# Paged attention in pairs of rounds instead of single rounds

## The chip, the core and the metric

The kernel runs on one core of a Trainium2 chip, in one launch. What is measured is the device time of that launch in microseconds; lower is better. TensorE (PE) multiplies matrices, VectorE (DVE) and ScalarE (ACT) do arithmetic on tiles, GpSimd (POOL) issues the gathers, and SyncE (SP) issues the other transfers.

## The reference, cut to what matters

The whole model is a state-space convolution, a causal attention, an attention over a paged cache, and a feed-forward layer with LoRA. The change touches only the paged attention:

```python
q, k, v = x @ Wq.T, x @ Wk.T, x @ Wv.T     # 32 entries of 32 tokens, 32 query heads, 8 key heads, D = 128
q, k = rope(rmsnorm(q)), rope(rmsnorm(k))
k_all = concat([k_cache[block_table], k])  # 16 pages of 32 keys, and 32 new keys: 544 keys
v_all = concat([v_cache[block_table], v])
scores = einsum(q, k_all) * SCALE          # four query heads to each key head
scores = where(valid, scores, -1e30)
o = softmax(scores) @ v_all
out = o @ Wo.T
```

Everything is float32.

## The kernel before, in words

`cached_attention` (lines 1232 to 1612) works on one batch entry and one key head at a time. That is a round: 128 query rows (4 heads of 32 tokens) against 544 keys. An entry has 8 rounds (k = 0 to 7), and a loop body has two entries, 16 rounds (i = 0 to 15); it is written out once for m = 0 and then looped 15 times. There are 256 rounds in all. Each engine has its own order of work, and semaphores join them.

A round passes through these steps:

- `split_hi` (ScalarE, L1401) copies the keys to a high part, and `split_lo` (VectorE, L1490) takes the rest as a low part. There are two buffers for each. At k = 1 and k = 4 the queries of the entry are split too (L1400 with 384 and 512 columns, L1487). Round k = 0 isn't split; it is multiplied in float32 (L1551).
- `scores` (TensorE, L450 to L452) has six matmuls: three products for each of two parts of the keys. The scores of even and odd rounds lie in one tile of three PSUM banks and share the middle bank. So each round computes its end part first, then waits until the mask of the round before is done, then computes its middle part.
- `mask_scores` (VectorE, L1501) adds the mask, moves the scores out of PSUM and takes the row minimum.
- `exponent` (ScalarE, L1406) and `normalise` (VectorE, L1508 and L1510).
- `transposes` (TensorE, L1570): four of 128 x 128 into `p_turn`, which has one buffer. Every fourth round the weights of the new keys of four rounds are transposed as well (L1576), from a copy that ScalarE gathers (`gather_new`, L1424).
- `take_turned` (ScalarE, L1414) copies `p_turn` to `probs_t`, and L1432 copies the new keys' part.
- `values` (TensorE, L1591): eight matmul instructions into `p_val`; after the eighth round 16 small ones for the new values (L1598). Then `take_values` (ScalarE, L1223) copies the finished entry out, SP stores it (L1228, L1229) and loads new values (L1341), and later the page keys of the entry after next (L879). POOL gathers value pages (L1353) after the values of an entry are done.

In a round i the TensorE order is scores(i), transposes(i - 3), values(i - 4). ScalarE does split_hi(i), gather_new(i - 4), take_turned(i - 5), exponent(i - 2); VectorE does mask(i - 2), split_lo(i), normalise(i - 3). The order is written out by hand in the functions called `body`.

Of the kernel before, what the change touches and what calls it, by code (L numbers as in the profile page):

```python
# [28 lines left out]
HQ, HK, D = 32, 8, 128  # L29
G = HQ // HK  # L30
# [1201 lines left out]
def cached_attention(nc, io, cst, x_res, wo, tables):  # L1232
# [5 lines left out]
    with ExitStack() as ctx:  # L1238
# [141 lines left out]

        def step_of(m, i, first, what):

            if i >= 0:
                what(m, i)
            elif not first:
                what(m - 1, RB + i)

        @block.scalar
        def _(act):
            def split_hi(m, i):  # L1390
                r = m * RB + i
                slot, k = i // HK, i % HK
                if k == 0:
                    return
                if k == 1:
# [5 lines left out]
                nc.scalar.activation(k_hi[:, i % 2, :].rearrange("p (n s) -> p n s", s=S), keys[slot][:, :, k, :], ACT.Copy).then_inc(k_hi_ready, 1)  # L1401
# [36 lines left out]

            def late(m, i):
                take_turned(m, i)  # L1440
                if i % NEW == NEW - 1:
                    take_turned_new(m, i // NEW)

            def later(m, i):
                if i % HK == HK - 1:
                    take_values(m, i // HK)

            def body(m, first):
                for i in range(RB):
                    split_hi(m, i)  # L1450
                    step_of(m, i - 4, first, gather_new)
                    step_of(m, i - 5, first, late)
                    step_of(m, i - 2, first, exponent)
                    step_of(m, i - 6, first, later)

            body(0, True)
            _loop(act, 1, B // 2, lambda m: body(m, False))
            for i in range(RB, RB + 6):
                if i - 4 < RB:
                    gather_new(LAST, i - 4)  # L1460
                if i - 5 < RB:
                    late(LAST, i - 5)
                if i - 2 < RB:
                    exponent(LAST, i - 2)
                if i - 6 < RB - 1:
                    later(LAST, i - 6)
                if RB < i <= RB + G:
                    act.wait_ge(wo_in, 16)
                    nc.scalar.activation(wo.hi[:, 0, i - RB - 1, :], wo.raw[:, 0, i - RB - 1, :], ACT.Copy).then_inc(wo_hi_ready, 1)

        @block.vector
        def _(v):
# [8 lines left out]
            def split_lo(m, i):  # L1481
                slot, k = i // HK, i % HK
                if k == 0:
                    return
                if k in QUERY_AT:
                    v.wait_ge(q_hi_ready, 4 * m + 2 * slot + (1 if k == 1 else 2))
                    v.tensor_tensor(q_lo[:, slot, QUERY_AT[k]], queries[:, slot, QUERY_AT[k]],  # L1487
                                    q_hi[:, slot, QUERY_AT[k]].bitcast(F32), ALU.subtract).then_inc(q_lo_ready, 1)
                v.wait_ge(k_hi_ready, splits_to(m, i))
                v.tensor_tensor(k_lo[:, i % 2, :].rearrange("p (n s) -> p n s", s=S), keys[slot][:, :, k, :],  # L1490
                                k_hi[:, i % 2, :].rearrange("p (n s) -> p n s", s=S).bitcast(F32), ALU.subtract).then_inc(k_lo_ready, 1)

            def mask_scores(m, i):
                r = m * RB + i
# [10 lines left out]
            def normalise(m, i):  # L1505
# [4 lines left out]
                v.tensor_scalar(probs[:, i % 8, :], probs[:, i % 8, :], inverse[:, i % 4:i % 4 + 1], None,  # L1510
                                ALU.mult).then_inc(probs_ready, 1)

            def body(m, first):
                for i in range(RB):
                    step_of(m, i - 2, first, mask_scores)
                    split_lo(m, i)
                    step_of(m, i - 3, first, normalise)
                    if i % HK == 0:
                        make_mask(m, i // HK)

            both(body, v)
            for i in range(RB, RB + 3):
                if i - 2 < RB:
                    mask_scores(LAST, i - 2)
                normalise(LAST, i - 3)
# [9 lines left out]

        @block.tensor
        def _(pe):
            def scores(m, i):
                r = m * RB + i
                slot, k = i // HK, i % HK  # L1540
                end, middle = ENDS[i % 2], MIDDLES[i % 2]
                if k == 0:
                    pe.wait_ge(kq_in[slot], LOADS * m + LOADS)
                else:
# [4 lines left out]
                def product(part):  # L1549
                    if k == 0:  # L1550
                        return pe.matmul(score_at(i % 2, part), queries[:, slot, 0:P],  # L1551
                                         keys[slot][:, part.start // S:part.stop // S, 0, :], start=True, stop=True)
                    return three_pass(pe, score_at(i % 2, part), q_hi[:, slot, k * P:(k + 1) * P], q_lo[:, slot, k * P:(k + 1) * P],
                                      k_hi[:, i % 2, part], k_lo[:, i % 2, part], True, True)

                if not (isinstance(r, int) and r < 2):
# [22 lines left out]
            def values(m, i):  # L1579
# [14 lines left out]
                if k == HK - 1:  # L1594
# [4 lines left out]
                                       start=False, stop=True, skip_group_check=True)  # L1599
                    mm.then_inc(new_done, 1)  # L1600

            def body(m, first):
                for i in range(RB):
# [5 lines left out]
            for i in range(RB, RB + 4):  # L1609
                if i - 3 < RB:  # L1610
                    transposes(LAST, i - 3)
                values(LAST, i - 4)


def output_ffn(nc, io, x_res, wo):
# [315 lines left out]
```

## Time and profile before

| | |
|---|---|
| median of 3 runs | 1692.99 us (1692.55 to 1693.76) |
| profiled execution, its own time | 1689.82 us |
| its span | 1687.6 us |
| PE busy | 1619.2 us (96%) |
| DVE busy | 1104.5 us (65%) |
| ACT busy | 943.1 us (56%) |
| POOL busy | 369.9 us (22%) |
| mean DMA rate over the span | 172 GB/s |
| paged attention | from 859.5 us (first scores) to 1475.4 us (first output product) |

The busy times are sums over stages that have different limits. The span is what the profiler recorded of one execution; the execution's own time is 2.2 us longer. A busy TensorE is not one at its peak, since the ends of matmuls are modelled. In a timeline row the first number is the start, the second the time until the last instruction of the row ends, and the text in brackets says how long the engine had been idle before it and who released it.

### The profile page before, as it was taken

The numbers are of one execution on the slowest core, as the hardware profiler recorded it, in microseconds if no ns is written. First come the engines' busy times: TensorE is split into PE (matmuls) and PEld (weight loads), VectorE is DVE, ScalarE is ACT, GpSimd is POOL, SyncE is SP. The second block draws the span as 40 slices with busy tenths as digits, with TensorE's granted clock in tenths as the row PEclk, the third lists the DMA queues.
The fourth block names the chain that finished last, engine by engine and source line by source line (L and its number), as shares of the span: only waits on it lengthen the run. The fifth ranks groups of instructions, "written<-read, shape, count | busy, mean of one in ns | idle before, by whom it ended". The sixth has DMA issues, their size and how long they took to land. (4 is left out here: it accounts for less than half of the span.)

```text
span 1687.6 us, 34168 instructions
## 1 busy us (share of the span) xinstructions
PE 1619.2 (96%) x10792; PEld 1404.1 (83%) x10792; DVE 1104.5 (65%) x2942; ACT 943.1 (56%) x2392; POOL 369.9 (22%) x370
## 2 busy tenths in 40 slices
PE   2899999999999999999979999999999999999998
PEld 2787888888888788888869999999999999977777
DVE  8405543454436657777768888888888888864443
ACT  3224323232222266766669989998899888822221
POOL 1000000000000246656532332223222322122210
PEclk9999999999999999999979999999999999999999
DMA  6621121110110433443578889988998898594301
GB/s 231 206 91 52 65 69 68 68 44 24 68 63 26 162 107 107 134 134 106 156 268 277 282 297 300 305 287 286 304 302 295 273 301 299 184 325 140 122 12 50
DMA packets 239311, 290.69 MB, mean 172 GB/s; under 512 B 18682, under 2 KB 182938, under 8 KB 239258
## 3 DMA queue, kind: packets, MB, share of 16 engines
q1 hardware_dynamic: 220826, 222.89, 39.8%
q0 software_dynamic: 18432, 67.12, 12.3%
q8 instruction: 30, 0.49, 0.1%
q14 instruction: 23, 0.19, 0.0%
HBM read 237.43 MB, written 50.41 MB: 171 GB/s over the span
## 5 line engine op out<-in xcount | busy, mean ns | idle before, releaser
L1591 PE MATMUL p_val<-probs_t,vals 128*128 128x128 f32 x2048 | 271.7, 276 | 1.7 <-DMA vals<-in_v_pages,rows_now 1.7
L1591 PEld LDWEIGHTS p_val<-probs_t,vals 128*128 128x128 f32 x2048 | 249.3, 192 | 2.0 <-DMA vals<-in_v_pages,rows_now 2.0
L1501 DVE CUSTOM_DVE_ANT_0 probs<-p_score,mask 128x544 f32<-128x544 f32 x256 | 184.3, 720 | 80.2 <-issue 77.6
L1406 ACT ACTIVATE probs<-probs,low 128x544 f32<-128x544 f32 x256 | 190.6, 745 | 0.3 <-DVE low L1501 0.3
L1060 POOL TENSOR_TENSOR w_lo<-w_raw,w_hi 128x512 fp32r<-128x512 f32 x44 | 57.7, 1316 | 548.4 <-DVE w_hi L1098 531.9
L1414 ACT ACTIVATE probs_t<-p_turn 128x512 f32<-128x512 f32 x256 | 149.5, 584 | 50.6 <-PE p_turn L1570 46.6
L450 PE MATMUL p_score<-wo_hi,q_hi 128*128 128x288 f32 x448 | 153.4, 342 | 11.9 <-DVE low L1501 11.3
L1490 DVE TENSOR_TENSOR wo_lo<-keys,wo_hi 128x544 fp32r<-128x544 f32 x224 | 161.7, 722 | 0.7 <-issue 0.7
L450 PE MATMUL p_tile<-w_hi,y_hi 128*128 128x512 f32 x384 | 156.9, 409 | 2.4 <-PEq L463 2.4
L1570 PE MATMUL p_turn<-cst,probs 128*128 128x128 f32 x1024 | 154.8, 274 | 3.2 <-issue 1.5
L1401 ACT ACTIVATE wo_hi<-keys 128x544 fp32r<-128x544 f32 x224 | 146.1, 652 | 17.6 <-PE p_score L452 12.9
L1353 POOL DMA_INDIRECT vals<-in_v_pages,rows_now x128 | 143.7, 1122 | 39.1 <-issue 31.2
L452 PE MATMUL p_tile<-w_hi,y_lo 128*128 128x512 f32 x384 | 150.9, 393 | 0.0
L451 PE MATMUL p_tile<-w_lo,y_hi 128*128 128x512 f32 x384 | 150.0, 391 | 0.0
L1510 DVE TENSOR_SCALAR probs<-probs,inverse 128x544 f32<-128x544 f32 x256 | 128.9, 504 | 9.1
L452 PE MATMUL p_score<-wo_hi,q_lo 128*128 128x288 f32 x448 | 129.9, 290 | 0.0
L451 PE MATMUL p_score<-wo_lo,q_hi 128*128 128x288 f32 x448 | 129.5, 289 | 0.0
L1039 ACT ACTIVATE squared<-p_tile 128x128 f32<-128x128 f32 x320 | 84.2, 278 | 77.9 <-PE p_tile L452 77.9
L450 PE MATMUL p_proj<-y_hi,w_hi 128*128 128x512 f32 x320 | 126.4, 395 | 0.2 <-DVE w_lo L689 0.2
L1570 PEld LDWEIGHTS p_turn<-cst,probs 128*128 128x128 f32 x1024 | 119.3, 141 | 8.6 <-issue 3.8
L1070 POOL TENSOR_TENSOR part_a<-part_a,part_b 128x512 f32<-128x512 f32 x80 | 103.5, 1294 | 99.5 <-DVE part_b L1140 97.2
L451 PE MATMUL p_proj<-y_lo,w_hi 128*128 128x512 f32 x320 | 124.7, 390 | 0.0
(216 smaller groups left out, 3604.4 us busy)
## 6 DMA issues: line engine op xcount, KB each, us to landing
keys<-in_k_pages SPq DMA_DIRECT2D x512, 128.0 KB
qk_new<-x_res SPq DMA_DIRECT2D x80, 256.0 KB, 2.3
x_res<-qk_new SPq DMA_DIRECT2D x32, 512.0 KB
o_new<-x_res SPq DMA_DIRECT2D x32, 512.0 KB
w_raw<-in_w_vkq_t SPq DMA_DIRECT2D x12, 1024.0 KB, 5.6
w_raw<-in_w_qkv_t SPq DMA_DIRECT2D x10, 1024.0 KB, 8.2
toep<-kpad SPq DMA_DIRECT2D x32, 256.0 KB, 4.9
w_raw<-in_w_dense_t SPq DMA_DIRECT2D x8, 1024.0 KB, 5.3
```

What stands on the lines that cost most here:

```text
L450: pe.matmul(out, a_hi, b_hi, start=start, stop=False)
L451: pe.matmul(out, a_hi, b_lo, start=False, stop=False)
L452: return pe.matmul(out, a_lo, b_hi, start=False, stop=stop)
L1353: pool.indirect_dma_start(to, None, source, bass.IndirectOffsetOnAxis(ap=rows, axis=0)).then_inc(done, 16)
L1401: nc.scalar.activation(k_hi[:, i % 2, :].rearrange("p (n s) -> p n s", s=S), keys[slot][:, :, k, :], ACT.Copy).then_inc(k_hi_ready, 1)
L1406: nc.scalar.activation(probs[:, i % 8, :], probs[:, i % 8, :], ACT.Exp, bias=low[:, i % 4:i % 4 + 1], scale=-1.0, accum_out=total[:, i % 4 ...
L1414: nc.scalar.activation(probs_t[:, i % 2, :, :], p_turn[:, :, :], ACT.Copy).then_inc(turned_taken, 1)
L1490: v.tensor_tensor(k_lo[:, i % 2, :].rearrange("p (n s) -> p n s", s=S), keys[slot][:, :, k, :], k_hi[:, i % 2, :].rearrange("p (n s) -> p ...
L1501: v.tensor_tensor_reduce(out=probs[:, i % 8, :], in0=score_at(i % 2, slice(0, KEYS)), in1=mask[:, i // HK, :], scale=1.0, scalar=3e38, op0 ...
L1510: v.tensor_scalar(probs[:, i % 8, :], probs[:, i % 8, :], inverse[:, i % 4:i % 4 + 1], None, ALU.mult).then_inc(probs_ready, 1)
L1570: mm = pe.transpose(p_turn[:, n, :], probs[:, i % 8, n * P:(n + 1) * P], ident)
L1591: mm = pe.matmul(p_val[:, h, half * P:(half + 1) * P], vals[:, slot, c, k * D:(k + 1) * D], probs_t[:, i % 2, c, :], start=(c == 0 and hal ...
```

## The change

TensorE now works in pairs of rounds. For even i the order is scores(i - 1), scores(i), transposes(i - 3), values(i - 4), transposes(i - 2), values(i - 3). The odd round computes its end part, waits for the even mask before it, and computes its middle part; the even round then computes its middle part first and its end part last. The completion of the odd round's scores is signalled by the even round's middle product. The split keys have four buffers instead of two; the two new ones lie in the part of `wo.hi` and `wo.lo` that the output weights use later, so the split of the output weights waits for all scores. ScalarE and VectorE are four rounds ahead of TensorE with the key splits. ScalarE's order in a pair is split_hi(i - 1), take_turned(i - 7), exponent(i - 5), split_hi(i), exponent(i - 4), gather_new(i - 5), take_turned(i - 6), take_values. The drain after the loop is rewritten to match. `step_of` returns when i is beyond the last round.

```diff
-        k_hi, k_lo = (a[:, 1, :, :].rearrange("p (r g) e -> p r (g e)", r=2)[:, :, 0:KEYS] for a in (wo.hi, wo.lo))
+        of_round = lambda a, i: a[:, i % 4 // 2, :, :].rearrange("p (r g) e -> p r (g e)", r=2)[:, i % 2, 0:KEYS]
+        k_hi, k_lo = (lambda i: of_round(wo.hi, i)), (lambda i: of_round(wo.lo, i))
...
-                if not (isinstance(r, int) and r < 2):
-                    act.wait_ge(scores_done, r - 1)
+                if not (isinstance(r, int) and r < 4):
+                    act.wait_ge(scores_done, r - 3)
...
+            def pair(m, i, first):          # ScalarE
+
+                step_of(m, i - 1, first, split_hi)
+                step_of(m, i - 7, first, late)
+                step_of(m, i - 5, first, exponent)
+                step_of(m, i, first, split_hi)
+                step_of(m, i - 4, first, exponent)
+                step_of(m, i - 5, first, gather_new)
+                step_of(m, i - 6, first, late)
+                if not (i - 7 == RB - 1 and not first):
+                    step_of(m, i - 7, first, later)
...
-                for i in range(RB):
-                    split_hi(m, i)
-                    step_of(m, i - 4, first, gather_new)
-                    step_of(m, i - 5, first, late)
-                    step_of(m, i - 2, first, exponent)
-                    step_of(m, i - 6, first, later)
+                for i in range(0, RB, 2):
+                    pair(m, i, first)
...
-            for i in range(RB, RB + 6):
...
+            for i in range(RB, RB + 8, 2):
+                pair(LAST, i, False)
+                if i >= RB + 4:
                     act.wait_ge(wo_in, 16)
-                    nc.scalar.activation(wo.hi[:, 0, i - RB - 1, :], wo.raw[:, 0, i - RB - 1, :], ACT.Copy).then_inc(wo_hi_ready, 1)
+                    act.wait_ge(scores_done, B * HK)
+                    for g in range(2):
+                        n = i - RB - 4 + g
+                        nc.scalar.activation(wo.hi[:, 0, n, :], wo.raw[:, 0, n, :], ACT.Copy).then_inc(wo_hi_ready, 1)
...
+            def pair(m, i, first):          # VectorE
+
+                step_of(m, i - 5, first, mask_scores)
+                step_of(m, i - 4, first, mask_scores)
+                step_of(m, i - 1, first, split_lo)
+                step_of(m, i - 5, first, normalise)
+                step_of(m, i, first, split_lo)
+                if i % HK == 0 and i < RB:
+                    make_mask(m, i // HK)
+                step_of(m, i - 4, first, normalise)
...
+            def odd_scores(m, i):
+                r = m * RB + i
+                operands(m, i)
+                if not (isinstance(r, int) and r < 3):
                     pe.wait_ge(masked, r - 1)
-                product(end)
-
-                if not (isinstance(r, int) and r < 1):
-                    pe.wait_ge(masked, r)
-                product(middle).then_inc(scores_done, 1)
+                product(m, i, ENDS[1])
+                pe.wait_ge(masked, r)
+                return product(m, i, MIDDLES[1])
+
+            def even_scores(m, i, first):
+                r = m * RB + i
+                operands(m, i)
+                done = product(m, i, MIDDLES[0])
+                if not (first and i == 0):
+                    done.then_inc(scores_done, 1)
+                product(m, i, ENDS[0]).then_inc(scores_done, 1)
...
+            def pair(m, i, first):          # TensorE
+
+                step_of(m, i - 1, first, odd_scores)
+                if i < RB:
+                    even_scores(m, i, first)
+                step_of(m, i - 3, first, transposes)
+                step_of(m, i - 4, first, values)
+                step_of(m, i - 2, first, transposes)
+                step_of(m, i - 3, first, values)
+
             def body(m, first):
-                for i in range(RB):
-                    scores(m, i)
-                    step_of(m, i - 3, first, transposes)
-                    step_of(m, i - 4, first, values)
+                for i in range(0, RB, 2):
+                    pair(m, i, first)
```

## Rows read from the trace of the kernel before

**Rows 1.** Windows: stretch, length, busy us (instructions) by engine, granted clock, DMA share, GB/s
```profile
873.00:876.20 3.20, 3.20 (x17) 3.20 (x17) 0.63 (x2) 0.64 (x2) 0.00 (x0) 0.50 1.04 410
...
900.00:1450.00 550.00, 536.46 (x4710) 515.57 (x4711) 469.44 (x1457) 490.14 (x1108) 154.55 (x203) 1.00 0.89 295
```

**Rows 2.** Timeline of PE: an ordinary round, and k = 0 scores of two entries
```profile
1102.33 0.38 PE L450 MATMUL p_score<-wo_hi,q_hi 128*128 128x288 f32 x1
...
1103.16 0.60 PE L1570 MATMUL p_turn<-cst,probs 128*128 128x128 f32 x4
1103.60 1.06 PE L1591 MATMUL p_val<-probs_t,vals 128*128 128x128 f32 x8
1104.41 0.38 PE L450 MATMUL p_score<-wo_hi,q_hi 128*128 128x288 f32 x1
...
1109.60 1.08 PE L1551 MATMUL p_score<-keys,x_res 128*128 128x288 f32 x4
...
1128.47 1.08 PE L1551 MATMUL p_score<-keys,x_res 128*128 128x288 f32 x4
```

**Rows 3.** Waits of PE and ACT, 900 to 1460 us: total, times, longest
```profile
PE p_score L450 <- DVE low L1501: 11.2, 28, 0.5
...
ACT probs_t L1414 <- PE p_turn L1570: 44.3, 33, 1.8
```

**Rows 4.** Timeline of all engines from 1105 us, in the thirteenth entry
```profile
1105.12 0.28 PE L452 MATMUL p_score<-wo_hi,q_lo 128*128 128x256 f32 x1
...
1105.24 0.60 PE L1570 MATMUL p_turn<-cst,probs 128*128 128x128 f32 x4
...
1107.03 0.72 DVE L1501 CUSTOM_DVE_ANT_0 probs<-p_score,mask 128x544 f32<-128x544 f32 x1 [1.64 <-issue]
...
1107.06 0.29 PE L452 MATMUL p_score<-wo_hi,q_lo 128*128 128x288 f32 x1
1107.08 0.60 ACT L1414 ACTIVATE probs_t<-p_turn 128x512 f32<-128x512 f32 x1 [1.65 <-PE p_turn L1570]
...
1107.81 0.38 PE L450 MATMUL p_score<-wo_hi,q_hi 128*128 128x256 f32 x1 [0.46 <-DVE low L1501]
```

**Rows 5.** Timeline of all engines in the last entry and its drain
```profile
1467.07 0.28 PE L452 MATMUL p_score<-wo_hi,q_lo 128*128 128x256 f32 x1
...
1467.40 0.72 DVE L1501 CUSTOM_DVE_ANT_0 probs<-p_score,mask 128x544 f32<-128x544 f32 x1 [0.96 <-issue]
...
1470.30 0.63 PE L1570 MATMUL p_turn<-cst,probs 128*128 128x128 f32 x4 [0.21 <-ACT probs_t L1414]
...
1470.97 0.60 ACT L1414 ACTIVATE probs_t<-p_turn 128x512 f32<-128x512 f32 x1
...
1471.71 0.63 PE L1570 MATMUL p_turn<-cst,probs 128*128 128x128 f32 x4
```

**Rows 6.** Timeline of ACT: the values of the entry before are taken
```profile
1100.34 1.03 ACT L1223 ACTIVATE x_res<-p_val 128x1024 f32<-128x1024 f32 x1
```

**Rows 7.** Timeline of ACT: starts one behind the other
```profile
1103.36 0.66 ACT L1401 ACTIVATE wo_hi<-keys 128x544 fp32r<-128x544 f32 x1 [0.23 <-PE p_score L452]
1103.92 0.29 ACT L1424 ACTIVATE probs_n<-probs 128x128 f32<-128x128 f32 x1
1104.12 0.58 ACT L1414 ACTIVATE probs_t<-p_turn 128x512 f32<-128x512 f32 x1
1104.60 0.74 ACT L1406 ACTIVATE probs<-probs,low 128x544 f32<-128x544 f32 x1
...
1114.88 0.63 ACT L1400 ACTIVATE q_hi<-x_res 128x512 fp32r<-128x512 f32 x1
1115.42 0.64 ACT L1401 ACTIVATE wo_hi<-keys 128x544 fp32r<-128x544 f32 x1
```

**Rows 8.** Timeline of PE and ACT in the first two entries
```profile
872.47 1.69 PE L1591 MATMUL p_val<-probs_t,vals 128*128 128x128 f32 x8 [1.72 <-DMA vals<-in_v_pages,rows_now]
...
882.32 0.52 ACT L1400 ACTIVATE q_hi<-x_res 128x384 fp32r<-128x384 f32 x1 [2.29 <-DMA keys<-in_k_pages]
```

More of the change, by code:

```diff
@@ L1381, in step_of @@
         def step_of(m, i, first, what):
+            if i >= RB:
+                return
             if i >= 0:
@@ L1396, in split_hi @@
                     act.wait_ge(kq_in[slot], LOADS * m + LOADS)
-                if not (isinstance(r, int) and r < 2):
-                    act.wait_ge(scores_done, r - 1)
+                if not (isinstance(r, int) and r < 4):
+                    act.wait_ge(scores_done, r - 3)
                 if k in QUERY_AT:
                     nc.scalar.activation(q_hi[:, slot, QUERY_AT[k]], queries[:, slot, QUERY_AT[k]], ACT.Copy).then_inc(q_hi_ready, 1)
-                nc.scalar.activation(k_hi[:, i % 2, :].rearrange("p (n s) -> p n s", s=S), keys[slot][:, :, k, :], ACT.Copy).then_inc(k_hi_ready, 1)
+                nc.scalar.activation(k_hi(i).rearrange("p (n s) -> p n s", s=S), keys[slot][:, :, k, :], ACT.Copy).then_inc(k_hi_ready, 1)
             def exponent(m, i):
@@ L1446, in later @@
                     take_values(m, i // HK)
-            def body(m, first):
-                for i in range(RB):
-                    split_hi(m, i)
-                    step_of(m, i - 4, first, gather_new)
-                    step_of(m, i - 5, first, late)
-                    step_of(m, i - 2, first, exponent)
-                    step_of(m, i - 6, first, later)
+            def pair(m, i, first):
[8 more added lines that the diff above has]
+                    step_of(m, i - 7, first, later)
+            def body(m, first):
+                for i in range(0, RB, 2):
+                    pair(m, i, first)
             body(0, True)
             _loop(act, 1, B // 2, lambda m: body(m, False))
-            for i in range(RB, RB + 6):
[L1459 to L1467, printed above, removed]
+            for i in range(RB, RB + 8, 2):
+                pair(LAST, i, False)
+                if i >= RB + 4:
                     act.wait_ge(wo_in, 16)
-                    nc.scalar.activation(wo.hi[:, 0, i - RB - 1, :], wo.raw[:, 0, i - RB - 1, :], ACT.Copy).then_inc(wo_hi_ready, 1)
+                    act.wait_ge(scores_done, B * HK)
+                    for g in range(2):
+                        n = i - RB - 4 + g
+                        nc.scalar.activation(wo.hi[:, 0, n, :], wo.raw[:, 0, n, :], ACT.Copy).then_inc(wo_hi_ready, 1)
         @block.vector
@@ L1489, in split_lo @@
                 v.wait_ge(k_hi_ready, splits_to(m, i))
-                v.tensor_tensor(k_lo[:, i % 2, :].rearrange("p (n s) -> p n s", s=S), keys[slot][:, :, k, :],
-                                k_hi[:, i % 2, :].rearrange("p (n s) -> p n s", s=S).bitcast(F32), ALU.subtract).then_inc(k_lo_ready, 1)
+                v.tensor_tensor(k_lo(i).rearrange("p (n s) -> p n s", s=S), keys[slot][:, :, k, :],
+                                k_hi(i).rearrange("p (n s) -> p n s", s=S).bitcast(F32), ALU.subtract).then_inc(k_lo_ready, 1)
             def mask_scores(m, i):
@@ L1511, in normalise @@
                                 ALU.mult).then_inc(probs_ready, 1)
-            def body(m, first):
-                for i in range(RB):
[L1515 to L1519, printed above, removed]
+            def pair(m, i, first):
[7 more added lines that the diff above has]
+                step_of(m, i - 4, first, normalise)
+            def body(m, first):
+                for i in range(0, RB, 2):
+                    pair(m, i, first)
             both(body, v)
[L1522 to L1525, printed above, removed]
+            for i in range(RB, RB + 6, 2):
+                pair(LAST, i, False)
             for g in range(G):
@@ L1537, in _, with product, operands @@
         def _(pe):
-            def scores(m, i):
-                r = m * RB + i
+            def product(m, i, part):
                 slot, k = i // HK, i % HK
-                end, middle = ENDS[i % 2], MIDDLES[i % 2]
+                if k == 0:
+                    return pe.matmul(score_at(i % 2, part), queries[:, slot, 0:P],
+                                     keys[slot][:, part.start // S:part.stop // S, 0, :], start=True, stop=True)
+                return three_pass(pe, score_at(i % 2, part), q_hi[:, slot, k * P:(k + 1) * P], q_lo[:, slot, k * P:(k + 1) * P],
+                                  k_hi(i)[:, part], k_lo(i)[:, part], True, True)
+            def operands(m, i):
+                slot, k = i // HK, i % HK
                 if k == 0:
@@ L1547, in scores @@
                     pe.wait_ge(k_lo_ready, splits_to(m, i))
[L1549 to L1556, printed above, removed]
-                    pe.wait_ge(masked, r - 1)
-                product(end)
-                if not (isinstance(r, int) and r < 1):
-                    pe.wait_ge(masked, r)
-                product(middle).then_inc(scores_done, 1)
+            def odd_scores(m, i):
+                r = m * RB + i
+                operands(m, i)
+                if not (isinstance(r, int) and r < 3):
+                    pe.wait_ge(masked, r - 1)
+                product(m, i, ENDS[1])
[8 more added lines that the diff above has]
+                product(m, i, ENDS[0]).then_inc(scores_done, 1)
             def transposes(m, i):
@@ L1600, in values @@
                     mm.then_inc(new_done, 1)
+            def pair(m, i, first):
[6 more added lines that the diff above has]
+                step_of(m, i - 3, first, values)
             def body(m, first):
-                for i in range(RB):
-                    scores(m, i)
-                    step_of(m, i - 3, first, transposes)
-                    step_of(m, i - 4, first, values)
+                for i in range(0, RB, 2):
+                    pair(m, i, first)
             both(body, pe)
[L1609 to L1612, printed above, removed]
+            odd_scores(LAST, RB - 1).then_inc(scores_done, 1)
+            for i in range(RB, RB + 4, 2):
+                step_of(LAST, i - 3, False, transposes)
+                step_of(LAST, i - 4, False, values)
+                step_of(LAST, i - 2, False, transposes)
+                step_of(LAST, i - 3, False, values)
 def output_ffn(nc, io, x_res, wo):
```

## The prediction

> **What bounds it now.** I read the windows first [rows 1]: from 900 to 1450 us, inside the paged attention, TensorE is busy 536 of 550 us at granted clock 1.00, ScalarE 490 (89%), VectorE 469 (85%). TensorE is the bound, but ScalarE has only a tenth of slack, so what matters is who stands ready when. Then TensorE's timeline. An ordinary round is scores 0.83, transposes 0.44, values 0.81, together 2.08 us [rows 2]. From the k = 0 scores of one batch entry to those of the next it takes 18.87 us. In it are 8 rounds (16.6), 4 x 0.22 us more that I read off the same timeline for the two extra transposes and the k = 0 product, 0.66 for the new tokens' values, and stalls. 18.1 us is left when the stalls are taken away.
>
> The stalls: the list of waits names one that counts, the mask (VectorE's score reduction), and one on ScalarE's side that is much larger, 44.3 us in 33 waits for the transposes [rows 3]. The timeline around 1105 us shows both as one event [rows 4]. The last score matmul starts at 1105.12, but the mask starts 1.91 us later; in the last batch entry the same pair is 0.33 apart [rows 5]. The transposes begin at 1105.24 and their copy at 1107.08, 1.84 later; when ScalarE is free that is 0.67 [rows 5]. VectorE and ScalarE both sat idle and both were let go at about 1107.05: TensorE's completion signals reached both late, all at one moment. That moment is 5.7 us after the end of the copy that takes the finished values of an entry (1100.34 + 1.03 = 1101.37) [rows 4, 6], when page gathers, output stores and the new-value load are all under way; the last entry, with no gather behind it, has no such event. I count it once per entry in the timeline, in 29 or 30 of 32. Today it costs TensorE 0.62 us: the second half of the scores starts 0.75 us after the third matmul of the first half (1107.06 and 1107.81 [rows 4]) instead of 0.13; the row itself shows 0.46 of it as idle.
>
> **The change part by part.** Number of instructions, shapes and DMAs stay the same; only the order, the number of split-key buffers (four for two) and the waits differ. So the sum is made of waits. I call a pair by its i modulo 8 on TensorE: pair 0 holds the scores of k = 7 and 0, pair 2 those of 1 and 2, and so on. In the steady state ScalarE and VectorE run the pair numbered four higher beside it.
>
> 1. The mask wait. The odd round's mask now has the four blocks behind it (transposes, values, transposes, values: 2.5 us) before the next scores need its bank. Even 1.6 us late it arrives in time. The 0.62 us goes: -0.62 per entry. Letting VectorE start the odd mask only after the even round's first product delays it by 0.36 us (three matmuls of 0.12), hidden by the same 2.5 us.
>
> 2. Transposes, values, transposes through one PSUM tile. Today values and a whole score block (0.81 + 0.83) stand between two uses of p_turn; in a pair it is values alone. The kernel's own tail has just this order with ScalarE free: transposes at 1470.30, their copy at 1470.97, next transposes at 1471.71 [rows 5]. That is 1.41 us against 0.44 + 0.81 = 1.25 by the ordinary round (some of the difference is only how the first score matmul is stamped). I take 0.12 per pair. Where the new keys' transpose (0.22) stands between, it is covered; that is pairs 2 and 6. So +0.24 per entry. Bounds: 0 and 4 x 0.16 = +0.64.
>
> 3. ScalarE's order in a pair: split, copy, exponent, split, exponent, gather, copy. Pitches [rows 7]: split 0.56, copy 0.48, exponent 0.74, gather 0.20, query split (512) 0.54, query split (384) 0.43 (0.52 [rows 8] less the 0.09 by which the larger one's next starts before its end). In pair 0 it also splits the later half of the queries. From the first transposes at t = 0: copy starts 0.67, exponent 1.15, query split 1.89, key split 2.43, exponent 2.98, gather 3.72, second copy 3.92, done 4.5, transposes could start at 4.65. TensorE gets there at 1.41 + 0.44 + 0.81 + two score blocks (1.58) = 4.25. Stall 0.4, once per entry: +0.38 by my finer walk. Bounds 0 (if ScalarE is a little ahead) and 0.6. In the other pairs the same walk ends before TensorE arrives.
>
> 4. The late signals. Their moment stays tied to the taking of the values, since gathers, stores and that load are all issued from there and SP's order is unchanged. The taking is now ScalarE's last act in pair 2 and ends about 1.3 us into pair 4. Pair 4 lasts 4.3 us, so 5.7 us later is 2.7 us into pair 6. There the scores' signal is due at 1.3 and the first transposes' at 2.2, and both come at 2.7. Then ScalarE first does what stands ahead of the copy: query split 0.43 and key split 0.56, for which it had waited for the scores; the copy takes 0.6, TensorE's start 0.14. The second transposes start at 4.4. TensorE, by scores 1.52, transposes 0.44, new 0.22, values 0.89, is there at 3.07. Stall 1.35, where today the copy has a score block to hide behind. Bounds: 0 (signals no longer late, or late elsewhere) and 1.9 (the event half a microsecond later).
>
> Queued behind that stalled ScalarE copy are the exponents of both heads, for which VectorE's normalise waits, and behind that the next pair's transposes; by the walk these end about 0.4 us before they are needed, so the delay doesn't grow.
>
> Per entry: -0.62 (and -0.1 of a wait for the copy of the new keys' weights, which now has a block more) + 0.24 + 0.38 + 1.35 = +1.25; rounding of my walk puts the entry at 19.99 us against 18.87, so +1.12. For 29 entries +32.5.
>
> 5. Start. The second entry's keys land at 882.3, and ScalarE waits for them with its split [rows 8]. That split is now two pairs ahead, and the copies of transposes 3 and 4 stand behind it. TensorE stops after values of round 2, where today it has scores, transposes and values of some more rounds done: one round (2.2) and 1.6 us until the copy is through, less the 0.5 it stalls today: +3.3. Long idling there should drop the clock once: it is at 0.50 from 873.0 to 876.2 [rows 1], just after the wait of 1.72 us at 872.47 [rows 8], and 3.2 us at half rate lose 1.6. I take +4.5; bounds 0 and 7. The end of the stage: one stall less in the drain (-0.4), the last entry without an event +0.4, and entry 1 +0.4.
>
> Other stages: the splits of the output weights move two pairs back in the drain, beside the last values; nothing, or 0.5 at most. SP and POOL: instructions and queue order unchanged; keys are wanted some 4 us sooner, and there is most of an entry's time (18.9 us) between issue and need.
>
> Sum: 32.5 + 4.5 + 0.4 = +37.4. The profiled execution took 1689.8 us (span 1687.6), so 1727; the median of the runs shown is 1693.0, 3.2 higher, so 1730 on the scale on which it is measured.
>
> **Rivals.**
> A. The late signals do no harm after the change, because their moment moves or a pair absorbs them. Then an entry is 18.9 - 0.72 + 0.62 - about 0.15 = 18.62, 31 x -0.25 = -7.8, with the start +4.5: 1690. For it: I know the event's time, not its cause. Against it: 5.7 us is the same to 0.1 in every entry that I looked at.
> B. Full gain: the events do no harm, ScalarE is ahead in pair 0 and the round trip costs nothing: -0.72 + 0.1 in 31 entries, +3 at the start: 1677. For it: TensorE is the bound and 18.1 us is the work. Against it: ScalarE at 89%, and the tail's 1.41.
> C. Half the stall: the event ends half a microsecond earlier in the pair, or ScalarE catches up: 1710.
> D. The clock falls. After each stall of 1.35 us the clock goes to 0.50 for 3.2 us, as after 872.47: +1.6 x 30 on top, 1778. Against it: the start was nearly idle before that, and the 0.5 us stalls of today leave the clock at 1.00 through 550 us.
> The Trainium skill, page "TensorE: Matmul & The Clock Gate", section "HAM oscillation", speaks for D: a kernel whose matmul bursts wait on something in every tile is throttled again in each. The trace agrees at 873 and not in today's attention; going by that rule alone the time would be D's.
>
> **Chances.** Forecast 0.60 (its own range 1714 to 1746), A 0.12, B 0.12, C 0.10, D 0.06. A measurement of this kernel tells about 0.2% (3.4 us) from no change. A lies on that edge and is split in two. Faster 0.12 + 0.05 = 0.17, same 0.07, slower 0.76. The range 1689 to 1750 leaves out B, D and a little of the forecast.
>
> **What would show it.** Right: in the waits of the attention, TensorE's transposes waiting for ScalarE's copy of p_turn, once per entry about 1.3 us and once about 0.4; the mask gone from TensorE's waits; TensorE at 92 to 94% in the attention's windows; 20.0 us from one entry's k = 0 scores to the next; the attention ending near 1512 instead of 1475. Wrong: entries under 18.9 us; a copy that starts promptly in every pair 6; a clock below 1.00 in the windows (then D); or a wait of the scores for split keys, which I hold to be impossible.

## The result, and the profile after

The kernel in pairs takes 1740.83 us (median of 4 runs, 1739.25 to 1741.4); the kernel before, run beside it, 1693.38. The ratio is 1.0274, 95% interval 1.0261 to 1.0287: slower by 47.5 us. The profiled execution has a span of 1738.4 us against 1687.6, 50.8 more.

The head of the profile, and its groups of instructions (busy, mean ns; idle time before, and what ended it):

```profile
PE 1627.3 (94%) x10792; PEld 1405.3 (81%) x10792; DVE 1117.9 (64%) x2942; ACT 944.2 (54%) x2392; POOL 363.1 (21%) x370
...
L1590 PE MATMUL p_turn<-cst,probs 128*128 128x128 f32 x1024 | 157.6, 277 | 56.4 <-ACT probs_t L1417 48.5 <-DVE probs L1517 7.1 <-issue 0.7
```

Before the transposes alone TensorE is idle for 56.4 us, 48.5 of it put down to ScalarE's copy. The windows of the attention (columns as in [rows 1]), with two short ones whose clock is told of below:

```profile
900.00:1450.00 550.00, 507.39 (x4386) 480.55 (x4385) 448.05 (x1353) 457.44 (x1030) 137.91 (x190) 1.00 0.81 274
...
880.60:887.40 6.80, 3.75 (x18) 3.78 (x19) 3.18 (x7) 4.21 (x10) 0.00 (x0) 0.51 1.07 337
1525.70:1529.10 3.40, 3.40 (x10) 2.68 (x9) 1.27 (x3) 0.47 (x2) 0.00 (x0) 0.53 0.46 174
```

Beside [rows 1], TensorE is busy 507 of 550 us where it was 536. The clock is still 1.00, and every engine and the DMAs do less per microsecond: nothing is saturated, the engines wait for each other. One batch entry, from its k = 0 scores to the next ones, takes 20.2 us, on average 20.34 over the last 29 intervals (20.27 without a single one of 22.33), where it was 18.91 (18.87 for the entry in [rows 2]):

```profile
1028.76 1.08 PE L1553 MATMUL p_score<-keys,x_res 128*128 128x256 f32 x4
1048.99 1.08 PE L1553 MATMUL p_score<-keys,x_res 128*128 128x256 f32 x4
```

The waits from 900 to 1500 us (total, times, longest), to be held against [rows 3]:

```profile
PE p_turn L1590 <- ACT probs_t L1417: 41.7, 30, 2.1
PE p_turn L1590 <- DVE probs L1517: 5.4, 29, 0.2
...
ACT probs_t L1417 <- remote: 50.1, 29, 1.8
...
DVE probs L1508 <- issue: 69.2, 60, 2.7
```

TensorE's wait for the mask (11.2 us in 28 times) is gone. In its place stands one for ScalarE's copy of the transposes: 41.7 in 30 is 1.39 each, once per entry. The timeline of all engines around one of them, in pairs 4 and 6 of an entry:

```profile
1058.30 1.03 ACT L1223 ACTIVATE x_res<-p_val 128x1024 f32<-128x1024 f32 x1
...
1061.21 0.63 PE L1590 MATMUL p_turn<-cst,probs 128*128 128x128 f32 x4
...
1062.49 0.38 PE L450 MATMUL p_score<-wo_hi,q_hi 128*128 128x288 f32 x1
...
1063.93 0.29 PE L452 MATMUL p_score<-wo_hi,q_lo 128*128 128x288 f32 x1
...
1064.87 0.60 ACT L1417 ACTIVATE probs_t<-p_turn 128x512 f32<-128x512 f32 x1 [1.78 <-remote]
1064.99 0.72 DVE L1508 CUSTOM_DVE_ANT_0 probs<-p_score,mask 128x544 f32<-128x544 f32 x1 [1.31 <-issue]
...
1065.36 0.52 ACT L1403 ACTIVATE q_hi<-x_res 128x384 fp32r<-128x384 f32 x1
...
1065.61 0.63 PE L1590 MATMUL p_turn<-cst,probs 128*128 128x128 f32 x4 [1.38 <-ACT probs_t L1417]
...
1066.32 0.59 ACT L1417 ACTIVATE probs_t<-p_turn 128x512 f32<-128x512 f32 x1
...
1067.19 0.60 PE L1590 MATMUL p_turn<-cst,probs 128*128 128x128 f32 x4
```

Pair 4's second transposes start at 1061.21. A free ScalarE copies them 0.67 later [rows 5], so at 1061.88; it starts at 1064.87, 3.0 us late, and VectorE's mask, whose scores had started at 1062.49, comes off at 1064.99. That is the moment of the late signals again: 5.54 us after the end of the taking (1058.30 + 1.03 = 1059.33), against 5.7 before. TensorE had finished pair 6's scores; their last matmul starts at 1063.93, so the transposes could start at about 1064.05. They write p_turn, which that copy still has to read, and wait until 1065.61: 1.56 late, of which the row shows 1.38 as idle.

The list of waits calls the copy's releaser "remote" and the mask's "issue", and neither names an engine. The trace also records every update of a semaphore, and these say whose lateness it is. TensorE's signals for pair 4's second transposes, for the values behind them and for the two scores of pair 6 come at 1064.77, 1064.86, 1064.96 and 1065.01. The matmuls behind these four start over a stretch of 2.7 us (1061.21 to 1063.93), their signals come within 0.24 us. So the matmuls had been done in time and only the signals were held back. An earlier one, of the values that start at 1060.19, came at 1062.58, some 1.3 late. ScalarE and VectorE meanwhile signalled on (six updates between 1061.8 and 1063.1). In e2 below, each of TensorE's signals comes about 0.3 us after the last matmul of its block starts. In this trace, in the kernel before and in e8, three to five signals are over 0.8 us late behind each of the first 30 of the 32 takings. Behind the last two, which have stores but no gather and no new-value load, none is.

### The profile page after: what moved, and what is told of

It is laid out like the page before. It is cut to its first block and busy times, and to the rows that moved or that the text cites. A ratio compares the mean times of both kernels' runs of the same rounds, so it can differ in the third digit from the quotient of the medians.

```text
span 1738.4 us, 33895 instructions
## 1 busy us (share of the span) xinstructions
PE 1627.3 (94%) x10792; PEld 1405.3 (81%) x10792; DVE 1117.9 (64%) x2942; ACT 944.2 (54%) x2392; POOL 363.1 (21%) x370
## 3 DMA queue, kind: packets, MB, share of 16 engines
q0 software_dynamic: 18432, 67.12, 11.2%
## 5 line engine op out<-in xcount | busy, mean ns | idle before, releaser
L1508 DVE CUSTOM_DVE_ANT_0 probs<-p_score,mask 128x544 f32<-128x544 f32 x256 | 175.8, 720 | 77.5 <-issue 74.6
L1590 PE MATMUL p_turn<-cst,probs 128*128 128x128 f32 x1024 | 157.6, 277 | 56.4 <-ACT probs_t L1417 48.5
L1590 PEld LDWEIGHTS p_turn<-cst,probs 128*128 128x128 f32 x1024 | 115.6, 141 | 78.7 <-issue 55.1
L450 PE MATMUL p_score<-wo_hi,q_hi 128*128 128x288 f32 (+1 forms) x448 | 141.5, 316 | 0.2
L1517 DVE TENSOR_SCALAR probs<-probs,inverse 128x544 f32<-128x544 f32 x256 | 133.9, 523 | 9.0
L1354 POOL DMA_INDIRECT vals<-in_v_pages,rows_now x128 | 131.1, 1024 | 39.0 <-issue 30.9
L451 PE MATMUL p_score<-wo_lo,q_hi 128*128 128x288 f32 (+1 forms) x448 | 129.7, 289 | 0.0
L452 PE MATMUL p_score<-wo_hi,q_lo 128*128 128x288 f32 (+1 forms) x448 | 129.3, 289 | 0.0
L452 PE MATMUL p_proj<-y_hi,w_lo 128*128 128x512 f32 x320 | 124.5, 389 | 0.0
```

Source lines behind the costliest of these rows:

```text
L450: pe.matmul(out, a_hi, b_hi, start=start, stop=False)
L451: pe.matmul(out, a_hi, b_lo, start=False, stop=False)
L452: return pe.matmul(out, a_lo, b_hi, start=False, stop=stop)
L1354: pool.indirect_dma_start(to, None, source, bass.IndirectOffsetOnAxis(ap=rows, axis=0)).then_inc(done, 16)
L1508: v.tensor_tensor_reduce(out=probs[:, i % 8, :], in0=score_at(i % 2, slice(0, KEYS)), in1=mask[:, i // HK, :], scale=1.0, scalar=3e38, op0 ...
L1590: mm = pe.transpose(p_turn[:, n, :], probs[:, i % 8, n * P:(n + 1) * P], ident)
```

## The experiments

**Two conditions.** The late signals are there on some occasions and not on others. The kernel before took 1690.7 to 1693.4 us in the runs beside the new kernel and beside the second group below, and 1667.6 and 1668.1 us (7 runs each) beside the first and the third. In all eight kernels profiled in those two groups no copy of ScalarE was late and the transposes' wait of 1.4 us was missing. The groups are e1 to e4, e5 to e8 and f1 to f4, and each ran on another chip, so no run tells whether the condition goes with the chip or with the time. Numbers are compared within a group only. e1, e2, e3, e6, f1 and f2 were executed once each, the others four times. e1, e3, f1 and f2 leave work out and compute wrong values.

My theory: the stall is the late moment, which now meets a copy that nothing hides. Rivals: the late moment is made by the stores, the gathers or the new-value load and can be moved; or ScalarE is simply behind, without any late signal.

**e1_gathers_none, e2_stores_shifted, e3_vnew_none.** Each takes away or moves one kind of DMA issued at the taking.

```
e1:  - for n in range(NPP // 4):
     + for n in range(NPP // 4 if first else 0):
     ...
     - pe.wait_ge(vals_gathered[slot], VALS * m + VALS)
     + pe.wait_ge(vals_gathered[slot], VALS)
e2:  - store(m - 1, slot)
     + if not (isinstance(m, int) and slot == 0):
     +     store(m - 2 + slot, 1 - slot)  # the output stores of one entry earlier
     + sp.wait_ge(out_ready, b - 1)
     ...
e3:  + if first:                      # ahead of the new-value load
     ...
     - pe.wait_ge(v_new_in[slot], 16 * m + 16)
     + pe.wait_ge(v_new_in[slot], 16)
```

> The new kernel, with the value pages gathered only for the first two batch entries (30 of 32 entries use stale values). The theory: once per entry TensorE's completion signals reach the other engines late, about 2.5 to 5.7 us after the finished values are taken, and this holds up ScalarE's copy of p_turn and by it TensorE's transposes for 1.4 us. If the page gathers cause the lateness, the 1.4 us wait goes in all entries: an entry takes 18.9 us instead of 20.27 and the kernel about 1697. If stores or the new-value load cause it, the wait stays and the time is 1735 to 1741. If it is mere transfer load, the wait shrinks to 0.5 to 1.0.

> The new kernel, with SP issuing the store of a finished entry almost an entry later (after the next entry's page keys, just before it waits for the next finished entry) instead of at once. If the stores cause the late signals, the late moment moves by about 13 us to some other pair, and TensorE's 1.4 us wait of the transposes behind taking the values goes or turns up elsewhere. If the gathers or the new-value load cause it, ScalarE still gets the signal of the second transposes of the pair 5.5 to 5.7 us after the values are taken, or about 1.1 us sooner if the new-value load, which is now issued sooner, causes it. Time 1741 then, within 5.

> The new kernel, with the new tokens' values loaded only for the first two entries (30 of 32 entries use stale ones). This transfer is small (128 partitions of 1 KB). If it causes the late signals the 1.4 us wait goes and the time is about 1697; if the gathers or stores do, the wait stays: 1741, within 5.

Measured: 1690.63, 1691.22 and 1693.03 us; before, 1667.58. An entry takes 18.69 us in all three. e4 kept all three kinds of DMA, ran beside them and had no late signals either, so their absence here says nothing of the cause. What these runs do show is the kernel without late signals, with its two other terms bare. TensorE and ScalarE in e2, from pair 0's two transposes to pair 2's first:

```profile
1020.30 0.60 PE L1594 MATMUL p_turn<-cst,probs 128*128 128x128 f32 x4
...
1021.68 0.63 PE L1594 MATMUL p_turn<-cst,probs 128*128 128x128 f32 x4
...
1024.16 0.58 ACT L1421 ACTIVATE probs_t<-p_turn 128x512 f32<-128x512 f32 x1
...
1024.40 0.29 PE L452 MATMUL p_score<-wo_hi,q_lo 128*128 128x288 f32 x1
...
1024.89 0.63 PE L1594 MATMUL p_turn<-cst,probs 128*128 128x128 f32 x4 [0.19 <-DVE probs L1521]
```

The round trip takes 1.38 (1020.30 to 1021.68). Pair 2's last score matmul starts at 1024.40 and its transposes could follow 0.12 later, at 1024.52; they start at 1024.89, 4.59 after pair 0's first (my walk said 4.65) and 0.73 after ScalarE's copy (the same 0.74 as in the tail, [rows 5]). So 0.37 is lost, by the two times to ScalarE, which comes behind in pair 0. The row shows half of it as idle and names VectorE, which e7 below contradicts.

**e4_copy_first.** ScalarE copies the first transposes before it splits keys.

```
-  step_of(m, i - 1, first, split_hi)
   step_of(m, i - 7, first, late)
+  step_of(m, i - 1, first, split_hi)
   step_of(m, i - 5, first, exponent)
```

> The new kernel, with ScalarE's first copy of p_turn ahead of the first key split in each pair. By the prediction's story of the 1.35 us (the late signals fall on the scores and first transposes of pair 6 and the copy stands behind two splits) the wait shrinks to 0.4: faster by 25 to 30 us. By the new trace's story (the late signal is that of pair 4's second transposes, whose copy is the last thing of the pair before) the 1.4 us stays, and since the split now begins 0.8 us later in each pair, ScalarE falls behind in pairs 0 and 6 by 0.9 and 0.6 us: slower by 30 to 50 us.

Measured: 1723.83 us, ratio 1.0331 (1.0314 to 1.0348); e1 to e3, on the same chip, took 1691 to 1693. An entry takes 19.75 against 18.69. ScalarE's two copies of pair 0, and pair 2's transposes:

```profile
1008.15 0.60 ACT L1417 ACTIVATE probs_t<-p_turn 128x512 f32<-128x512 f32 x1 [0.81 <-PE p_turn L1590]
...
1011.92 0.58 ACT L1417 ACTIVATE probs_t<-p_turn 128x512 f32<-128x512 f32 x1
...
1012.65 0.63 PE L1590 MATMUL p_turn<-cst,probs 128*128 128x128 f32 x4 [0.74 <-DVE probs L1517]
```

ScalarE sits idle 0.81 us for the transposes and does the split afterwards, so the second copy comes 3.77 after the first and TensorE waits 0.74. Here ScalarE, with a tenth of slack, could not afford to wait in front of a ready instruction. The late-signal part of the expectation could not be tested.

**e5_after and e6_before.** Both kernels unchanged, as the measure for this group.

> The new kernel once more, unchanged, beside the kernel before on one chip. On the chip of the last four runs no completion signal of TensorE was late in any kernel, the kernel before took 1667.6 us, and entries took 18.69 us in variants of the new one. If the late signals belong to the chip or the occasion and not to gathers, stores or loads: with them 20.27 us an entry, 1741 against 1693 (+2.8%); without them 18.7 us an entry, about 1691 against 1668 (+1.4%). Only these two, nothing between.

> The kernel before, unchanged, for its trace on this chip. Without late signals the mask wait of 0.62 us is gone and an entry takes 18.1 to 18.2 us (1668 in all); with them 18.87 (1693). That the second entry starts at 882 to 883 us while the new kernel's starts at 887 to 888 holds either way.

Measured: 1739.72 us, ratio 1.0286 (1.0269 to 1.0303), and 1692.74. Waits from 900 to 1450 us, first e5, then e6:

```profile
PE p_turn L1590 <- ACT probs_t L1417: 36.3, 27, 2.1
```

```profile
PE p_score L450 <- DVE low L1501: 9.6, 27, 0.5
...
ACT probs_t L1414 <- PE p_turn L1570: 41.9, 39, 1.8
```

The late signals are in both, and both repeat the picture: 0.36 a time for the mask before, 1.34 for the copy after. One part of the expectation for e6 failed: its second entry starts at 885.0, not at 882 to 883, and e5's at 888.7, so the start costs 4.4 us in this pair of profiles (28.64 against 24.24 for the first interval).

**e7_copy2_first.** ScalarE copies the second transposes ahead of the even round's exponent.

```
+  step_of(m, i - 6, first, late)
   step_of(m, i - 4, first, exponent)
   step_of(m, i - 5, first, gather_new)
-  step_of(m, i - 6, first, late)
```

> The new kernel, with ScalarE's second copy of p_turn ahead of the second exponent (and of the gather of the new keys' weights) in each pair. By the theory that ScalarE's backlog after pair 0 (it splits the larger half of the queries there) makes pair 2's first transposes wait 0.37 us, this wait goes: 0.37 x 31 = 11.5 us faster than the new kernel on the same chip, 18.3 us an entry without late signals. If that wait is VectorE's normalise, as the list of waits says, nothing changes. With late signals present the 1.4 us stays, since the copy still waits for them.

Measured: 1717.55 us, ratio 1.0156 (1.0139 to 1.0173), 22 us less than e5; an ordinary entry takes 19.43 where e5's takes 20.23. The waits and one event:

```profile
PE p_turn L1590 <- ACT probs_t L1417: 25.0, 28, 2.0
...
ACT q_hi L1403 <- PE p_score L452: 32.9, 23, 1.7
```

```profile
1060.99 0.38 PE L450 MATMUL p_score<-wo_hi,q_hi 128*128 128x288 f32 x1
...
1063.49 0.52 ACT L1403 ACTIVATE q_hi<-x_res 128x384 fp32r<-128x384 f32 x1 [0.72 <-PE p_score L452]
1063.92 0.64 ACT L1404 ACTIVATE wo_hi<-keys 128x544 fp32r<-128x544 f32 x1
1064.47 0.58 ACT L1417 ACTIVATE probs_t<-p_turn 128x512 f32<-128x512 f32 x1
1065.19 0.63 PE L1590 MATMUL p_turn<-cst,probs 128*128 128x128 f32 x4 [0.89 <-ACT probs_t L1417]
```

The wait put down to VectorE's normalise is gone, though VectorE's work was not touched: it was the copy. With the second copy earlier, pair 4's is done before the late stretch, and what is caught is the chain that I had predicted: query split, key split, copy, then pair 6's second transposes. An entry gains 0.80: 0.37 that was ScalarE's backlog of pair 0, and 0.43 by the smaller stall. That is twice the gain that I expected, and the expectation that the 1.4 us would stay was wrong.

**e8_store_shifted.** e2's kernel, where the late signals are present.

> The new kernel with the stores of a finished entry issued almost an entry later, once more. Where the new kernel in this call shows late signals: if the stores cause them the 1.4 us wait behind pair 4 goes or moves, and the time falls by 25 to 45 us; if not, the same time within 5. Where there are none, the same time within 3 as the new kernel.

Measured: 1739.18 us, ratio 1.0282 (1.0265 to 1.0299). Its waits:

```profile
PE p_turn L1594 <- ACT probs_t L1421: 38.1, 27, 1.5
...
ACT probs_t L1421 <- remote: 46.5, 26, 1.9
```

The wait of 1.4 us is where it was, so the output stores don't make the signals late. The run says something of the new-value load too. With no store ahead of it SP issues this load 0.17 us after the taking, where it was 1.44. The expectation for e2 said that the late moment would then come about 1.1 us sooner if the load were its cause. The late copies start 5.55 us after the taking on average, against 5.51 in the new kernel and 5.46 in e5. That speaks against the load. The gathers were issued at the same moments in all three.

**f1_gathers_none and f2_vnew_none.** e1 and e3 once more, meant for a chip with late signals.

> The new kernel, with the value pages gathered for the first two batch entries only (30 of 32 use stale values), once more, for a chip on which signals are late: the first try was on one where none were. Gathers cause them: 18.7 us an entry, 1691. The new-value load or the mere occasion cause them: 20.2 to 20.3 us an entry, 1735 to 1741. If the unchanged order shows none here either (seen from the other runs of this call), it says nothing.

> The new kernel, with the new tokens' values loaded for the first two entries only (30 of 32 use stale ones), once more for the same reason. Gathers cause the late signals: 20.2 to 20.3 us an entry. This small load causes them: 18.7 us an entry, 1691 to 1693.

Measured: 1693.29 and 1691.03 us, before 1668.13, and no late signals in any kernel of the group. Inconclusive.

**f3_gather_later.** The value gathers wait for two more copies.

```
   pool.wait_ge(val_done, (b - 1) * HK)
+  pool.wait_ge(turned_taken, (b - 1) * HK + 2)
```

> The new kernel, with the gathers of an entry started about 3.2 us later, when ScalarE has copied the first transposes of pair 4. If the gathers cause the late signals, the late stretch moves with them, from 3.6 us into pair 4 to about 2.5 us into pair 6, between the signal of its first transposes and that of its second; the second copy then waits to 5.6 and TensorE 0.1 to 0.5 us instead of 1.4: 28 to 40 us faster than the new kernel, 1700 to 1712. If the stretch starts a little sooner than that it takes the first transposes too and the wait is over 2 us: slower than 1741. If the new-value load causes them, nothing moves and the time stays within 5 of 1740. On a chip without late signals: 1691, as the unchanged one.

Measured: 1692.11 us (1690.87 to 1696.42), ratio 1.0147 (1.0126 to 1.0168). An entry takes 18.69, as in e1 to e3, so the wait costs nothing; whether it would move the late signals stays open. Gathers unmoved cost the same in e2, so the ratio stands for the cost of the change where there are no late signals; the new kernel unchanged was never run there.

**f4_gather_later_mixed.** f3, with e7's order in pair 0 only.

```
+  if i % HK == HK // 2:
+      step_of(m, i - 6, first, late)
   step_of(m, i - 4, first, exponent)
   step_of(m, i - 5, first, gather_new)
-  step_of(m, i - 6, first, late)
+  if i % HK != HK // 2:
+      step_of(m, i - 6, first, late)
```

> The same with, besides, ScalarE's second copy ahead of the second exponent in the pair in which it also splits the larger half of the queries, and only there. That takes the 0.37 us behind pair 0: 0.37 x 31 = 11.5 us faster than the run before it, so 1688 to 1700 with late signals (against 1691 to 1693 for the kernel before) and about 1680 without (against 1668). If the move of the gathers does nothing, 1728.

Measured: 1679.91 us, ratio 1.0063 (1.0046 to 1.0080). Two k = 0 scores, 18.35 apart (18.27 and 18.35 in turn, 18.31 on average):

```profile
1000.86 1.08 PE L1557 MATMUL p_score<-keys,x_res 128*128 128x256 f32 x4
1019.21 1.08 PE L1557 MATMUL p_score<-keys,x_res 128*128 128x256 f32 x4
```

From 900 to 1450 us the list of waits has no row left for TensorE. An entry is 0.38 shorter than f3's: over 31 entries 11.8 us, and the medians differ by 12.2. No version that I tried beat the kernel before.

## Why the prediction came out as it did

1. **The mask's wait: right.** It is gone from TensorE's waits in the attention in every version.

2. **The round trip through one PSUM tile: right.** 1.38 in e2 against the 1.41 used.

3. **ScalarE's backlog in pair 0: right.** Predicted 0.38, read 0.37; moving one copy took 12 us away (f3 to f4).

4. **The late signals: the wrong victim, and a size 0.2 too small.** Predicted was a stall of 1.35 at pair 6's *second* transposes; it came at its *first*. I had the end of the late stretch (about 5.7 us after the taking) and assumed that it was some 1.8 us long, because no wait before was longer than that [rows 3]. It is longer: the copy at 1064.87 was due at 1061.88. In the rows that I had read of the kernel before, no signal was due early in the stretch. Its trace has one: TensorE's signal for the values that start at 1103.60 was due at about 1104.7 and came at 1106.91, but no engine was waiting for it, so that no wait shows it. e7, in which pair 4's second copy is done sooner, has the stall where I had put it, with 0.89 of idle time in its rows. So the predicted sum held partly by luck: the copy itself was late by about as much as the queue ahead of it would have cost.

   Idle time in the rows (1.39 a time) is not quite the measure that I had predicted in. Step by step, an ordinary entry of the new kernel lies beside e2's to 0.01 us up to these transposes, and is 1.58 behind from there on (20.23 against 18.65). In the kernel before, the score block of the late moment takes 1.56 where an ordinary one takes 0.83 [rows 2], 0.73 more (the prediction's 0.62 and 0.1):

```profile
1106.71 0.38 PE L450 MATMUL p_score<-wo_hi,q_hi 128*128 128x288 f32 x1
...
1108.27 0.60 PE L1570 MATMUL p_turn<-cst,probs 128*128 128x128 f32 x4
```

   That this term needs the late signals is shown by the two conditions: 47 to 49 us of slowdown with them, 24 without. 1.58 less 0.73 is 0.85, and over 30 takings that is 25 us, against a difference of 23 to 25.

   Per entry: predicted +1.12, measured 1.43 (29 intervals, 41.45 us more). Of the 0.31 between them 0.23 is this stall (1.58 against 1.35), and 0.07 the single entry of 22.33.

5. **The start: right.** Predicted +4.5, measured +5.25 (the first interval of k = 0 scores is 28.06 against 22.81) and +0.21 in the second; between e5 and e6 it is 4.4. TensorE and ScalarE there:

```profile
872.03 1.16 PE L1611 MATMUL p_val<-probs_t,vals 128*128 128x128 f32 x8 [2.35 <-DMA vals<-in_v_pages,rows_now]
...
881.95 0.52 ACT L1403 ACTIVATE q_hi<-x_res 128x384 fp32r<-128x384 f32 x1 [7.12 <-DMA keys<-in_k_pages]
...
883.65 1.08 PE L1590 MATMUL p_turn<-cst,probs 128*128 128x128 f32 x4 [6.08 <-ACT probs_t L1417]
```

   The keys land when they did before [rows 8]; ScalarE, which wants them two pairs earlier, now stands still 7.12 us where it stood 2.29, with finished transposes behind the split in its queue. TensorE idles 6.08 us and its clock is at 0.51 from 880.6 to 887.4: its 3.75 busy us there cost about 1.9 more than at full rate, an estimate by the two clock levels. In e4, where the copies stand ahead of the splits, the first interval is 22.81 again; but the second takes 22.79 where e2's takes 18.73, so most of the loss only comes later.

6. **The end of the stage: missed.** I had booked it near nothing. From the last entry's k = 0 scores to the first product of the output stage it takes 27.67 us against 24.98, +2.7. TensorE, VectorE and ScalarE there:

```profile
1497.12 1.08 PE L1553 MATMUL p_score<-keys,x_res 128*128 128x256 f32 x4
...
1518.50 0.31 ACT L1427 ACTIVATE probs_n<-probs 128x128 f32<-128x128 f32 x1 [0.77 <-DVE probs L1517]
...
1519.44 0.63 PE L1590 MATMUL p_turn<-cst,probs 128*128 128x128 f32 x4 [0.77 <-ACT probs_t L1417]
...
1522.01 0.73 PE L1618 MATMUL p_val<-probs_nt,vals_new 32*128 32x128 f32 x16
1523.18 1.28 DVE L1540 TENSOR_TENSOR wo_lo<-wo_raw,wo_hi 128x512 fp32r<-128x512 f32 x2
...
1524.79 0.48 PE L450 MATMUL p_out<-wo_hi 128*128 128x512 f32 x1 [2.06 <-PEq L1238]
```

   In the drain there are no scores between the transposes, so the gather of new weights, which stands ahead of a copy, waits for VectorE's normalise (0.77). In e7, where that copy stands ahead of the gather, the stage's end takes 26.99. The split of the output weights slides past the last values, and the output product waits 2.06: it starts 0.33 after VectorE's last split ends (1524.46), where in the kernel before it started 0.35 after TensorE's own last values. I had allowed 0.5 at most. The clock is at 0.53 for the 3.4 us after it. The attention ends at 1524.8, not near 1512.

The sum: 5.25 + 0.21 + 41.45 + 2.7 = 49.6 of the 50.8 us by which the spans differ. The part of 41.45 above 32.5, 9 us, is the largest error; 2.1 of it is a single entry, 22.33 long (1413.83 to 1436.16), in which that stall took 2.10 and the clock was at 0.50 from 1433.3 to 1436.7.

**The rivals.** A, that the late signals do no harm, is what a chip without them gives, but it put the new kernel's entry at 18.62 and the kernel before stands lower there too: the change stays slower by 1.47% (f3). B fails at the backlog and the round trip. C asked for half a stall; it was whole, and a little more. D would have needed the clock to fall after each stall. With 1.4 us of idling in every entry the windows still give 1.00 over 550 us. It did fall around the 6.08 us at the start and behind the one stall of 2.10 us, so D was wrong for stalls of this size and not for all. The Trainium skill (page "TensorE: Matmul & The Clock Gate", section "HAM oscillation") describes a kernel that waits for its data in every tile and is throttled anew in each. The trace agrees at the start (0.51), and not in the attention's once-per-entry stall of 1.4 us (1.00).

**Left open.** What makes TensorE's signals late, and why only in one of the two conditions. The stores are excluded where the lateness was present (e8), and the last two takings, which have only stores, show none. The value gathers and the new-value load were taken away only where it was absent. Issuing the load 1.27 us sooner did not move the late moment (e8), which leaves the gathers as the likelier of the two; that they are the cause is not shown.

## What to carry to other kernels

When work is regrouped into larger units, walk every in-order queue once in the steady state, once at the first entry and once in the drain; here start and end cost 8 us that had nothing to do with the regrouping's own gain. A queue that must wait for a transfer should not have finished work of others behind it. Where a stall was short, ask what hid it: the late signals cost 0.7 us an entry while a score block stood between two uses of a PSUM tile, and 1.6 once it was gone. A signal that nobody waits for can be late without showing in any wait; the record of semaphore updates has it.

## What the runs showed of the hardware

TensorE's completion signals can come up to 3.0 us late, three to five of them together, once per batch entry, until 5.5 to 5.7 us after the values are taken, while its matmuls and the signals of ScalarE and VectorE go on. It happens on one occasion and not on another with the same program, the kernel before. That kernel gains 25 us without it (1693 to 1668, 1.5%), the kernel in pairs about 48 (1740 to the 1692 of f3). Compared on different occasions, the kernel before with late signals (1693) and the kernel in pairs without (1692) would have looked equal, so each was timed beside the kernel before.

A wait that has several conditions is put down to one engine, and it can be the wrong one: 0.37 us lost to ScalarE's copy was listed as 0.19 "DVE probs", and late TensorE signals as "remote" and "issue". Moving one instruction settled the first, the record of semaphore updates the second.
